# Where the last self-attention block's values, statistics and norm stand as self-attention hands over to cross-attention

## The reference

```
y  = layernorm(x)                                   # no gain
y  = layernorm(y + attention(y, y, y, causal)) * g1 + beta1
y  = layernorm(y + attention(y, Z, Z)) * g2 + beta2  # Z: the context, 1601 rows
y  = layernorm(y + relu(y @ w1 + b1) @ w2 + b2) * g3 + beta3
x1 = x + y
out = x1 + mixture_of_experts(layernorm(x1))        # 8 experts, the best 2 of each row, silu-gated
```

## Time and profile before

| | |
|---|---|
| median of three runs | 547.83 us |
| profiled execution | 549.44 us |
| its span, first to last instruction | 547.7 us |
| mean granted TensorE clock | 0.992 of full speed |
| busy: PE, DVE, ACT, POOL | 91%, 70%, 52%, 54% of the span |
| self-attention's last scores, cross tile 0's last scores | end at about 105 us, 109 us |
| biases of cross tiles 1, 2, 3, 4 start at | 118.05, 126.87, 136.26, 145.02 us |

### The profile page before, as it was taken

One profiled execution on the slowest core, in us unless ns is written; L12 is line 12 of the kernel. 1 busy time (PEld: TensorE's weight loads), 2 busy tenths in 40 slices (PEclk: granted clock), 3 DMA queues, 4 the chain that ended last, 5 costly groups with the idle time before them and its releaser, 6 DMA issues.

```text
span 547.7 us, 11131 instructions
## 1 busy us (share of the span) xinstructions
PE 500.6 (91%) x3734; PEld 329.3 (60%) x3734; DVE 383.6 (70%) x974; ACT 286.8 (52%) x588; POOL 295.8 (54%) x332
## 2 busy tenths in 40 slices
PE   7999999989999998899899978679999999999990
PEld 3676766756676664566565667445565656666660
DVE  5899886688778579868886887987867544444440
ACT  4647867564749455764357383474554343443430
POOL 3565031005544349645885659653647676667673
PEclk9999999999999999999999999999999999999996
DMA  8011614238895356964768433126796898987883
GB/s 270 10 49 49 200 61 144 89 73 147 155 165 125 95 111 114 200 154 97 127 158 197 155 82 117 48 71 111 135 164 102 118 131 122 131 118 135 130 95 37
DMA packets 135316, 65.63 MB, mean 120 GB/s; under 512 B 109757, under 2 KB 126590, under 8 KB 135262
## 3 DMA queue, kind: packets, MB, share of 16 engines
q1 hardware_dynamic: 127774, 54.69, 46.8%
q0 software_dynamic: 7488, 10.23, 12.9%
HBM read 28.19 MB, written 10.35 MB: 70 GB/s over the span
## 4 chain that ended last, share of the span: by engine, by line
PE 51%; DVE 17%; ACT 9%; DMA 8%; issue 7%; POOL 5%; POOLq 1%; SPq 0%; DVEq 0%; ACTq 0%
PE ps L1157 40%; DMA out<-y,qst 5%; ACT ps L974 3%; DVE cmax L1681 3%; PE ps L1252 3%; PE ps L1254 3%; PE ps L1253 3%; ACT prob L973 3%; DMA probT<-prob 2%; DVE arena L370 1%; DVE prob L1822 1%; POOL out L928 1%; PE ps L1456 1%; POOL y L816 1%; DVE arena L439 1%
## 5 line engine op out<-in xcount | busy, mean ns | idle before, releaser
L1157 PE MATMUL ps<-arena,probT 128*128 128x256 f16 (+2 forms) x1092 | 180.1, 318 | 5.1 <-DMA probT<-prob 2.9
L1157 PEld LDWEIGHTS ps<-arena,probT 128*128 128x128 f16 (+1 forms) x1092 | 104.7, 97 | 63.0 <-issue 7.4
L973 ACT ACTIVATE prob<-ps,nbias 128x512 f16<-128x512 f32 x64 | 39.0, 610 | 79.1 <-DVE nbias L1687 79.1
L928 POOL DMA_INDIRECT out<-y,qst x39 | 62.5, 1603 | 24.7 <-DMA out<-y,qst 11.7
L1157 PE MATMUL ps<-arena,qT 128*128 128x512 f16 (+1 forms) x384 | 69.2, 332 | 6.8 <-DVE prob L1822 6.8
L2217 DVE SCALAR_TENSOR_TENSOR ps<-ps,w1m 128x512 f32<-128x512 f32 x39 | 27.3, 699 | 55.4 <-ACT w1m L1100 55.3
L1100 ACT ACTIVATE w1m<-ps 128x512 f32<-128x512 f32 x39 | 23.3, 597 | 74.7 <-PE ps L1157 74.7
L1157 PE MATMUL ps<-arena,tT 128*128 x468 | 57.4, 273 | 0.6 <-DVE tT L2312 0.6
L1157 PEld LDWEIGHTS ps<-arena,qT 128*128 128x128 f16 x384 | 32.5, 97 | 41.8 <-issue 8.2
L1157 PE MATMUL ps<-w2s,tT 128*128 128x256 f16 x384 | 48.2, 273 | 5.4 <-DVE tT L1890 5.1
L1822 DVE TENSOR_TENSOR prob<-ps,prob 128x512 f16<-128x512 f32 x64 | 36.1, 571 | 23.0 <-ACT ps L974 22.9
(11 more groups left out here) (220 smaller groups left out, 968.5 us busy)
## 6 DMA issues: line engine op xcount, KB each, us to landing
stage<-we_in SPq DMA_DIRECT2D x33, 256.0 KB, 3.0
prob<-we_in SPq DMA_DIRECT2D x15, 256.0 KB, 3.2
xin<-x_in SPq DMA_DIRECT2D x16, 128.0 KB, 2.8
out<-y SPq DMA_DIRECT2D x16, 128.0 KB
hrow<-tT SPq DMA_DIRECT2D x4, 512.0 KB
y<-x_in SPq DMA_DIRECT2D x3, 512.0 KB, 7.2
stage<-z_in SPq DMA_DIRECT2D x4, 256.0 KB, 5.5
prob<-w_in SPq DMA_DIRECT2D x4, 256.0 KB, 2.9
```

Of the source, the lines that this page charges most:

```text
L928: g.indirect_dma_start(out[:rows_of(p), :], bass.IndirectOffsetOnAxis(ridx[:, n:n + 1], 0), ys[:, n % RING, :], None, compute_op=ALU.add). ...
L973: a.activation(row_cols(q, 0, c), ps[c][:, :w], ACT.Exp, bias=nbias[:, q, :], scale=SM)
L1157: r = t.matmul(o, lhs(a), rhs(b), start=first and n == 0, stop=last and n == 2)
```

## The change

Three things are moved; nothing is added or removed.

1. PE: the value products of group 33 (12 matmuls) go behind the two chunks of tile 0's scores (12 matmuls of 512 columns) that used to follow them.
2. DVE: c_max of tile 0's last two chunks and c_bias(0) go ahead of inverse and add_to_y of the last block, and these are mixed otherwise with c_los of tile 0 and c_max of tile 1.
3. DVE: s_stats of the last block goes from ahead of step 0 to the end of step 0, and s_norm from the end of step 0 to the end of step 1.

```
-                if s >= LAG:
+                if LAG <= s < NG - 1:
                     s_pv(s - LAG)
             c_scores(0, (0,), True)
             c_scores(0, (1,), True)
+            s_pv(NG - 3)
             s_pv(NG - 2)
             s_pv(NG - 1)
...
-            inverse(NB - 1, 0)
             c_max(0, 0, 0)
-            add_to_y(NB - 1, 0)
             c_max(0, 0, 1)
             c_bias(0, 0)
+            inverse(NB - 1, 0)
+            add_to_y(NB - 1, 0)
+            c_los(0, 0)
             inverse(NB - 1, 1)
+            add_to_y(NB - 1, 1)
+            c_los(0, 1)
             inverse(NB - 1, 2)
-            add_to_y(NB - 1, 1)
             inverse(NB - 1, 3)
             add_to_y(NB - 1, 2)
-            c_los(0, 0)
+            c_max(1, 1, 0)
+            c_los(0, 2)
             add_to_y(NB - 1, 3)
-            for c in range(1, C_CH):
-                c_los(0, c)
-                c_max(1, 1, c - 1)
+            c_max(1, 1, 1)
+            c_los(0, 3)
+            c_max(1, 1, 2)
             q_lo(2)
             c_max(1, 1, C_CH - 1)
             c_bias(1, 1)
-            s_stats(NB - 1)
             sums("c_", 0, C_CH, 0, C_CH)
             q_lo(3)
...
                 if i == 0:
+                    s_stats(NB - 1)
+                if i == 1:
                     s_norm(NB - 1)
```

## The result

The changed kernel took 556.18 us in the median of 6 runs (554.15 to 560.62), the kernel before 547.66 (545.94 to 548.66, 6 runs): a ratio of 1.014, 95% interval 1.0103 to 1.0176. That is slower, as forecast, but above the forecast range (550.9 to 554.6). Measured twice more beside the kernel before, the changed kernel stood at 553.41 against 546.75 (1.0119, 1.0084 to 1.0154) and 553.11 against 546.64 (1.0094, 1.0060 to 1.0128); both of these times lie inside the forecast range. Medians here are of all executions, while the ratios leave out the slow ones (four of e7_norm0_first's twelve, one each of e3_bias_first's and e5_filler's) and are not quotients of the medians. The profiled execution took 554.57 us, with a span of 552.8.

What follows compares the result with a forecast made beforehand. DVE's 8.8 us loop bound cross-attention, then PE alone up to 191.5 us. Gains up to bias 3 were included; SP's late transposes left +4.85 us on the 547.83 median, giving 552.7 us, range 550.9 to 554.6.

Steps and rivals of the forecast that it cites:

- The third part, SP's wait: s_norm one step later holds SP's overwriting (L638) until 142.1, so later transposes delay tile 5's scores by 4.85 us.
- The landing of the last transpose: turn(3, 2), issued at 147.95, was taken to land 4.0 us later, ahead of PE's last 15 value products.
- POOL beneath SP: residual(2) waits for POOL until about 143.85, bias 4 comes 2.9 us later, but SP's longer delay hides this.
- POOL's stall alone: Rival: SP catches up and only residual(2)'s wait for POOL remains, about +2.7 us, 550.5 us; chance 0.13.
- The first two parts up to bias 3: Earlier bias 0 and moved s_stats on DVE bring bias 3 to 135.4 from 136.26, 0.85 us early.
- the case that kept this gain: Rival: s_norm is hidden, SP's wait ends before turn(3, 0) is due, and the gain stays: 546.6 us; chance 0.05.
- which I had put at nothing since SP would be blocked: On DVE, s_norm beside a weight's low half delays tile 3's first low half by up to 1 us, at no cost.
- The clock: Rival: PE's idle time before tile 3's value products brings half clock, +3 us more, 555.7 us; chance 0.08.
- the prediction's own signs of being wrong: L638 issued by 136, PE's +4.85 shift shrunk by the first feed-forward block, or clock below 1.00 near 145 to 155.
- so nothing takes it back: PE alone is on the chain behind tile 5's scores up to 191.5 us, so the +4.85 us reaches the end.

Runs made afterwards that it cites:

- e7_norm0_first: Changed kernel with POOL's norm of cross tile 0 ahead of s_affine, SP's wait kept: 555.28 us, ratio 1.0082.
- e3_bias_first: Changed kernel with s_stats and s_norm put back, so only the first biases and value products reordered: 548.32 us, ratio 1.0000.
- e5_filler: Changed kernel plus 24 idle-time matmuls on PE, into a bank nothing reads, in its two idle times: 552.96 us, ratio 1.0099.
- r_filler: Changed kernel plus the same 24 idle-time PE matmuls, measured a second time: 553.78 us against 546.75, ratio 1.0133.
- e2_norm_alone: Kernel before with one edit, s_norm at the end of step 1 instead of step 0: 556.73 us, ratio 1.0177.
- e1_reload_later: Changed kernel with SP overwriting gain and shift in step 3 instead of step 1: 551.39 us, ratio 1.0070.
- e6_both_later: Changed kernel with SP's overwriting in step 3 and POOL's norm of cross tile 0 ahead of s_affine: 546.80 us, ratio 1.0005.
- e9_norm_halves: Changed kernel, SP's overwriting in step 3, s_affine behind cross tile 2's norm, s_norm halved over steps 1 and 2: 547.10 us, ratio 1.0009.
- a_changed: The changed kernel unaltered, measured a third time: 553.11 us against 546.64, ratio 1.0094.
- The filler kernels: Changed kernel plus 24 idle-time PE matmuls in its two idle times, measured three times: 552.96, 553.78 and 554.40 us.
- a_before: The kernel before measured against itself, for scatter and a second profile: 546.56 us against 546.64, ratio 0.9989.

## Why the prediction was right and wrong

**The third part, SP's wait: right.** It forecast L638 at 142.1 and turn(3, 1) at 146.6; the profile has 142.87 and 147.04 (with its late 0.9 us), r_filler 142.13 and 146.31. Tile 5's scores were forecast at 153.6, +4.85; three profiles with the clock held have 153.37 to 153.48. e2_norm_alone shows that this move alone loses, e1_reload_later and e6_both_later that the two waits for s_affine are its only ways. The landing of the last transpose was put at 4.0 us: it was 4.04 in r_filler, but 5.45 in the profile of the changed kernel, a term sized too low there by 1.45.

**POOL beneath SP: right.** residual(2) ran at 144.80, or 143.9 without the lateness, as forecast. The rival *POOL's stall alone*, priced at 550.5, is what e1_reload_later made: 551.39.

**The first two parts up to bias 3: right in size, wrong in worth.** Bias 3 was forecast at 135.4 and came at 136.17, or 135.3 without the lateness; the wait for tile 1's last transpose is gone. But the case that kept this gain was priced at 546.6, -1.2; e6_both_later and e9_norm_halves keep it, win 0.1 to 0.5 us at tile 5's scores (148.41 and 148.23 against 148.51 and 148.76), and end with no measurable gain. The step left out was that s_norm beside a weight's low half keeps turn(3, 1) near its old time (140.34 against 140.50), which I had put at nothing since SP would be blocked.

**The clock: the step that failed at the place.** It was a rival with 0.08, argued from the end of the trace, where PE had stood idle through 536 to 538 at the full level, and the sum had no term for it. In all three profiles of the changed kernel it fell, on two idle times of 2.5 and 2.8 to 3.0 us with 0.36 us of work between; a clock below 1.00 near 145 to 155 was one of the prediction's own signs of being wrong. It belonged in the forecast, with 0 to 2.3 us at tile 5's scores, and not with the +3 that the rival gave it, since a landing can hide it. The Trainium skill, in "TensorE: Matmul & The Clock Gate", section "Why this matters for your kernels", asks for no idle gaps of TensorE between bursts of matmuls, since it goes back to half clock. By that rule the rival was the likely case, and the trace agrees behind these two waits (0.50 in a_changed), though not behind every wait of this length (tile 10 of the kernel before, 1.00).

**The end: the other step that failed, with its cause open.** The sum took the +4.85 us at tile 5's scores for the whole loss at the end, "so nothing takes it back". Nothing did, but something was added. The filler kernels, whose clock stood, had +4.6 to +5.0 us at tile 5's scores and +4.6 to +4.7 at bias 9 (216.15 to 216.25 against 211.52 and 211.58), and ended +5.7 to +7.8 over before. Over all executions the changed kernel and the filler both end at +6.8, 2 us above the forecast. So the range's top of 554.6 (+6.8) lay in the middle of what was measured, and the first measurement, +8.5, lay above it. That the next two lay inside the range is scatter and no merit of the sum. The profiles place the excess of the filler behind cross-attention: from PE's last routing matmul (L1401 in the kernel before, L1408 with the filler) to its last matmul of all they took 129.1 to 130.1 us, against 125.3 to 126.8 in the five profiles that don't lose (before, a_before, e3_bias_first, e6_both_later, e9_norm_halves). But the changed kernel's took 126.0, 130.7 and 126.4. I can't tell scatter of the experts' part from an effect of the change, and no run told it apart.

A slip in the sum changes nothing: +6.0 us on 547.83 is 553.8, where the prediction's own range has 554.0 as its top.

## What to carry to other kernels

When work moves later, look for every queue whose next row waits on its last result, and count from there what stands behind the row: here an overwriting whose reader on POOL comes 30 us later held six issues, and cost more than the moved work itself took. Idle times of PE of 2.4 to 3 us cost clock in some executions here and not in others, and a landing that follows can hide the cost; keep the clock in the forecast, as a range, where a change gives PE idle time that it had not. A shift that is right at the place need not be the shift at the end, so forecast both. A gain upstream of a transfer is worth no more than what it moves that transfer's issue.

## What the runs showed of the hardware

The half level outlasted the idle time that brought it: in a_changed the clock was 0.50 in every window from 146 to 156, though PE was busy for all of 148 to 150 and 152 to 156. The same wait brought the half level in one execution and not in another: at tile 10 the 24 score matmuls took 4.24 us behind an idle time of 2.39 in before, and 5.88 behind 2.43 in a_before, where the clock was 0.53 in 216 to 218. With 24 matmuls into an unread bank the level stayed at 1.00 from 140 to 160, in four profiles of four. The later transposes of a burst could land late: turn(3, 2) of the changed kernel took 5.45 us and turn(3, 1) of a_changed 5.03, against a median of 3.4, while turn(3, 2) of r_filler took 4.04. DVE's s_norm instructions took 0.40 to 0.41 us each in e6_both_later and 0.48 and 0.88 in e9_norm_halves, where POOL was working. s_affine's first instruction took 2.73 us beside DVE's weight half, against 2.35; I had not looked for that. It shows in no lateness of L638, which came 6.63 us behind s_norm's start (136.24 to 142.87), against 6.58 before, where SP still had an issue of its own under way.
